# A narrower tile of row maxima in a four-layer attention kernel: 32 columns for a turning matmul instead of 128

## What is computed

```
q, k, v = norm(x) @ w + b            # 256 places, 12 heads of 16
s = q @ k.T * scale + bias           # per head 256 x 256
out = softmax(s) @ v                 # per head
x = x + out @ wo + bo
```

## Time and profile before

| what | value |
|---|---|
| three runs | 171.93, 172.28, 172.29 us; median 172.28 |
| the profiled execution | 172.13 us, of which the span from first to last instruction is 170.3 us |
| PE busy | 158.2 us, 93% of the span |
| DVE, ACT, POOL busy | 86.4, 70.4, 45.3 us |
| granted TensorE clock, mean | 0.997 of 2.4 GHz |

### The profile page before, as it was taken

How to read it: one execution, slowest core, us unless ns; L and a number is a source line. 1 busy time by engine, 2 the same in 40 slices (tenths; PEclk the granted TensorE clock), 3 DMA queues, 4 the chain that set the end, 5 groups by cost and what they waited for, 6 DMA issues and landing times.

```text
span 170.3 us, 2785 instructions
## 1 busy us (share of the span) xinstructions
PE 158.2 (93%) x1012; PEld 104.9 (62%) x1023; DVE 86.4 (51%) x224; ACT 70.4 (41%) x162; POOL 45.3 (27%) x73
## 2 busy tenths in 40 slices
PE   6899999999798999999979998989999899989991
PEld 2488667656455757655548755767665588666650
DVE  3554449735432979784340034385345434297462
ACT  5363307761222126780254422356632052256720
POOL 7699384520279174000000000430000061000000
PEclk9999999999999999999999999999999999999998
DMA  4705636999013952000000000710000027220001
GB/s 108 187 31 147 192 108 190 295 300 228 12 9 26 220 162 69 0 4 0 0 0 0 0 0 4 217 61 0 6 0 0 0 91 212 71 94 4 2 0 46
DMA packets 11825, 13.18 MB, mean 77 GB/s; under 512 B 3810, under 2 KB 9938, under 8 KB 11811
## 3 DMA queue, kind: packets, MB, share of 16 engines
q1 hardware_dynamic: 8402, 10.51, 21.3%
q0 software_dynamic: 2960, 2.09, 5.8%
q10 hardware_dynamic: 448, 0.39, 0.8%
HBM read 6.43 MB, written 0.20 MB: 39 GB/s over the span
## 4 chain that ended last, share of the span: by engine, by line
PE 82%; DVE 9%; ACT 4%; issue 2%; POOL 0%; DVEq 0%; ACTq 0%; POOLq 0%
PE PC L977 12%; PE RING L952 9%; PE RING L847 7%; PE PB L988 7%; PE RING L916 4%; PE PB L847 4%; PE RING L890 3%; PE RING L1171 3%; PE PA L1177 3%; PE PB L865 3%; DVE NM L759 3%; PE RING L892 2%; PE PA L1062 2%; PE PB L916 2%; PE PC L881 2%
## 5 line engine op out<-in xcount | busy, mean ns | idle before, releaser
L580 ACT ACTIVATE PR<-RING 128x512 f32<-128x512 f32 (+1 forms) x48 | 25.9, 554 | 9.5 <-PE RING L952 9.1
L847 PE MATMUL RING<-WARM 128*128 128x512 bf16 x99 | 27.1, 402 | 1.8 <-POOL WARM L359 1.3
L977 PE MATMUL PC<-PR,VX 128*32 128x256 f32 (+1 forms) x192 | 23.9, 368 | 0.0
L759 DVE TENSOR_REDUCE NM<-RING 128x2 fp32r<-128x512 f32 (+1 forms) x32 | 20.4, 653 | 4.7 <-PE RING L916 4.5
L952 PE MATMUL RING<-QS,KS 128*128 128x256 f32 (+1 forms) x96 | 20.3, 305 | 0.2
L952 PEld LDWEIGHTS RING<-QS,KS 128*128 128x128 f32 x96 | 14.0, 189 | 7.4 <-issue 4.4
L847 PEld LDWEIGHTS RING<-WARM 128*128 128x128 bf16 x108 | 10.2, 106 | 10.7 <-issue 1.9
L572 ACT ACTIVATE QS<-PA 4x512 fp32r<-4x512 f32 (+1 forms) x20 | 10.6, 532 | 11.6 <-PE PA L930 11.5
L759 DVE TENSOR_REDUCE NM<-PB 128x2 fp32r<-128x512 f32 (+1 forms) x16 | 10.5, 655 | 8.3 <-PE PB L916 8.1
L977 PEld LDWEIGHTS PC<-PR,VX 128*32 128x32 f32 x192 | 9.3, 109 | 8.2 <-ACT PR L580 1.7
L916 PE MATMUL RING<-KS,QS 128*128 128x256 f32 (+1 forms) x64 | 13.4, 297 | 0.6 <-DVE NM L759 0.6
(11 more groups left out here) (169 smaller groups left out, 267.8 us busy)
## 6 DMA issues: line engine op xcount, KB each, us to landing
WQKV<-in_w SPq DMA_DIRECT2D x2, 576.0 KB, 8.8
WO<-in_wo SPq DMA_DIRECT2D x4, 288.0 KB, 8.7
W<-in_ff SPq DMA_DIRECT2D x2, 576.0 KB, 9.5
WQKV<-in_w SPq DMA_DIRECT2D x2, 432.0 KB, 4.8
KS<-KH SPq DMA_DIRECT2D x4, 192.0 KB, 3.4
QS<-QHL POOLq DMA_DIRECT2D x12, 64.0 KB, 3.2
QS<-RH SPq DMA_DIRECT2D x12, 64.0 KB, 2.0
QS<-RL SPq DMA_DIRECT2D x12, 64.0 KB, 2.0
```

Source lines behind the costliest of these rows:

```text
L580: A(PR[:, h % NPR, 0:n], exponents(l, h)[:, 0:n], ACT.Exp).then_inc(sem("probs"), 1)
L759: V.tensor_reduce(NM[:, TURN_OF[h], :, h % GH], MAXIMA[h % 3][:, 0:2 * n_keys].rearrange("p (q k) -> p q k", q=2), AX.X, ALU.max, negate=T ...
L847: M(bank, WARM[:, 0:P], WARM[:, :], start=True, stop=True)
L977: ins = M(columns(h)[:, reach(l, k)], VX[:, k, h, :], half(PR[:, h % NPR, :], l, k), start=(k == 0 and l != 2), stop=(k == 1), skip_group_ ...
```

## The change

A slot of `NM` has 32 columns instead of 128, and so has the stationary operand of the turning matmul, which now writes partitions 0 to 31 of its bank instead of all 128. ACT reads the first four of them, as before. The program gives such a matmul a tile of 128 rows x 32 columns of the array, at column 0, where the former had the whole array. The two fills of `NM` on GpSimd shrink from 768 to 192 columns each. No instruction is added, removed or moved.

```
-        NM = sb("NM", [P, len(TURNS), 2, P], F32R)
+        NM = sb("NM", [P, len(TURNS), 2, 32], F32R)
...
-                    ins = M(turn_bank(t)[:, q * P:(q + 1) * P], NM[:, t, q, :], IDR[:, :], start=True, stop=True)
+                    ins = M(turn_bank(t)[0:32, q * P:(q + 1) * P], NM[:, t, q, :], IDR[:, :], start=True, stop=True)
```

## The result

| | before | after |
|---|---|---|
| median of 20 runs | 172.17 us | 171.06 us |
| range | 171.44 to 178.49 | 170.53 to 172.4 |
| span of the profiled execution | 170.3 us | 169.7 us |

The ratio of the changed kernel to the former is 0.9941, with a 95% interval of 0.9923 to 0.9958: 1.0 us less, where the forecast had 3.2 us more, 175.3.

A forecast was written before the change was run, and what follows sets the result against it. The prediction took PE to bound the kernel, so turns are paid almost everywhere. Layer terms of 0.9, 0.8, 0.66 and 0.85, together 3.2 us, added to the profiled 172.13 gave 175.3 us, range 173.7 to 176.4.

The forecast's parts named there:

- What bounds the kernel, and what a turn costs before: PE bounds the kernel, with 82% of the chain; a turn costs 0.23 us of a 0.69 us window, paid in weight loads.
- What it adds: Two changes of matmul kind per turn, 48 in all, each with 0.09 to 0.10 us of standing still.
- I take them for the form 128*32 and not for L977.: Extra times around L977 were read as belonging to any 128*32 matmul: 0.09 to 0.10 us each way.
- The rule: Changing the tiling mode drains TensorE, read as 0.09 to 0.10 us each way; a turn becomes 0.90 to 0.91 us.
- The size of the term: 0.2 us more per turn; by layers 0.9, 0.8, 0.66 and 0.85, together 3.2 us.
- The saved load time ... can't be had: At the turns, loads shorter by 0.16 us per turn gain nothing, since no load runs across the change of kind.
- the shorter load wins: Rival: loads around the turn hide as now, streams bound it at 0.59 us, 0.10 less per turn; 170.4 us, chance 0.04.
- no standing still: Rival: 32 columns at column 0 are entered and left without a gap, 0.70 against 0.69 us; 172.1 to 172.3, chance 0.05.
- More passes: Rival: narrow fp32r makes two passes like L977, each turning matmul 0.215 us instead of 0.055; 181.7 us, chance 0.02.
- The fills on GpSimd at nothing: Fills before layer 0 shrink from 1.53 us, but POOL has no share in the chain; costed at nothing, bounds 0.2.
- Results of a turn 0.11 later: A turn's results come about 0.11 us later, by 0.10 for the way in and the unhidden load.
- What would show it wrong: Signs against the forecast: L930 starting at 0.23 us behind its pair, or the pairs behind it keeping 0.29.

## Why the prediction was wrong

- **What bounds the kernel, and what a turn costs before: right.** The turns stand in PE's chain, twenty of them before and eighteen in the profiled execution of the change. That 0.05 us per turn times twenty gives just the 1.0 us of the medians is in part chance, since the profiled stretches show 0.55 and 0.67 and one layer lost its share to a transfer.
- **The step that failed is under "What it adds": "I take them for the form 128*32 and not for L977."** I gave as the reason that the rows come out the same whatever the data type. They didn't show that: in each of them the side with 32 columns was fp32 (L977), and only the other side varied. The rule put at 0.2 us per turn what the changed turn does not pay: it is 0.64 long where the forecast had 0.90. The one narrow matmul in fp32r that the trace had, L881, paid nothing, and I put that down to its 64 columns. Type and width were confounded in the trace, and I took the wrong one. The runs separate them: bf16 with 64 columns pays, fp32 and bf16 with 32 pay, fp32r with 4, 32, 64 and 96 does not. Why fp32r is free of it stays open.
- **The size of the term was right where the mechanism exists.** Sum 3.2 us, 175.3; the bf16 turn of 32 columns took 174.99, and by layers 0.80, 1.05, 0.57 and 0.74 more than before against 0.9, 0.8, 0.66 and 0.85.
- **"The saved load time ... can't be had": wrong with it,** but half of it is not to be had for another reason: the first of the two loads was hidden before. The rival "the shorter load wins" had the right side and took 0.10 per turn and 170.4; it is 0.05 and 171.06, since it let the 128-column load behind the turn hide as in an undisturbed stream, whereas the pair behind still takes 0.29 (28.43 to 28.72). Its chance of 0.04 was far too small for a reading that a row of the trace, L881's, spoke for.
- **The rival "no standing still"** was the right description (172.1 to 172.3 forecast), and its price was wrong: its 0.35 for the pair behind takes the load to be unhidden, as behind L977.
- **"More passes" was rightly refuted:** one record per matmul, 0.06 apart.
- **The fills on GpSimd at nothing: right,** shown by the wide tile with the narrow matmul.
- **Results of a turn 0.11 later: wrong;** its second matmul ends 0.05 sooner (222 against 275 ns).
- **What would show it wrong** was named: L930 at 0.23 behind its pair. It is at 0.24, and the pair behind it keeps its 0.29, which was the other sign named.

## What to carry to other kernels

Before a cost is moved from one instruction to another, list in what they differ, the data type with the shape; rows that agree only because they all share one property say nothing on it, and the odd row that disagrees deserves a run of its own or a large chance. In this kernel, a stationary operand narrower than the array was free of charge between matmuls on the whole array if both operands were fp32r. Narrowing it helped until its load was shorter than the stream before it, and no further (64, 32 and 4 columns gave the same). A visit to 32 columns cost 0.22 us net in bf16 (0.88 against 0.66) and 0.30 in fp32 (1.22 against 0.92). In a stream of matmuls with short moving operands, count the loads: a further pair with 128 columns cost 0.24 us by its loads, where its streams take 0.12.

## What the runs showed of the hardware

- Going from matmuls on 128 columns to ones on 32 (fp32, bf16) or 64 (bf16) and back makes TensorE stand still about 0.09 us each way, and leaves the load behind uncovered (windows 0.88 to 1.22); in fp32r it does not (0.64), although the program names the same tile size. The Trainium skill (TensorEngine Tiling (Array Packing), Key Properties) says that changing the tiling mode drains the engine; these runs agree for fp32 and bf16, where the engine stands still for those 0.09 us, and an fp32r matmul from column 0 behaves as if it changed nothing. Why is not shown; that the narrow fp32r matmul is run in the mode of the whole array would fit all runs.
- Where it stands still, the column position makes no difference to the windows (1.22 and 1.21 at columns 0 and 32; 183.15 and 183.61 us, of which 0.2 is a longer wait for a transfer).
- fp32r and bf16 loads of 128 columns differ (188 and 97 ns in the records of L930), and the short one is worth as much as a narrow fp32r operand: 171.29 and 171.06 us.
